# Rank products of two token groups later in the attention loop, the third group routed by VectorE, both halves of the second expert weights loaded behind the loop

## The reference

```python
h = mod(x_flat[:, :2].sum(axis=1).astype(int32), 8)     # route of each token
sel = stack([h, mod(h + 1, 8)], axis=1)                 # two experts per token
# for each expert e: acc += 0.5 * (relu(x @ W1[e] + b1[e]) @ W2[e] + b2[e]) where e in sel
```

## Time and profile before

| | us |
|---|---|
| median of 3 runs | 357.28 |
| lowest and highest | 352.55, 359.18 |
| the profiled execution | 350.9 |
| its span | 349.1 |
| PE busy | 267.8 (77%) |
| DVE busy | 174.5 (50%) |
| ACT busy | 152.4 (44%) |
| POOL busy | 121.7 (35%) |

### The profile page before, as it was taken

How to read it: one execution, slowest core, us unless ns; L and a number is a source line. 1 busy time by engine, 2 the same in 40 slices (tenths; PEclk the granted TensorE clock), 3 DMA queues, 4 the chain that set the end, 5 groups by cost and what they waited for, 6 DMA issues and landing times. The chain is left out here.

```text
span 349.1 us, 7349 instructions
## 1 busy us (share of the span) xinstructions
PE 267.8 (77%) x2443; PEld 205.1 (59%) x2443; DVE 174.5 (50%) x612; ACT 152.4 (44%) x367; POOL 121.7 (35%) x213
## 2 busy tenths in 40 slices
PE   0798966589699977898887969721078999999990
PEld 0587755345486755354545445421066999999990
DVE  4640656910315677787783913166001565665650
ACT  2234124438668664577673653301016343434430
POOL 4000015503305324264074553756000443534441
PEclk9999999879989999899997885555569999999997
DMA  7800005601998645278500000402792000000000
GB/s 215 261 6 1 0 5 142 127 0 47 227 182 257 145 110 93 77 151 202 125 3 18 18 4 25 128 8 84 157 243 61 8 23 15 17 15 15 7 15 13
DMA packets 30546, 28.34 MB, mean 81 GB/s; under 512 B 2846, under 2 KB 27041, under 8 KB 30515
## 3 DMA queue, kind: packets, MB, share of 16 engines
q1 hardware_dynamic: 28900, 25.24, 30.4%
q0 software_dynamic: 1328, 2.66, 2.3%
q10 hardware_dynamic: 288, 0.07, 0.1%
HBM read 17.85 MB, written 10.37 MB: 81 GB/s over the span
## 5 line engine op out<-in xcount | busy, mean ns | idle before, releaser
L980 ACT ACTIVATE CTX<-ps 128x512 f32<-128x512 f32 x64 | 37.5, 601 | 34.9 <-PE ps L656 27.1
L1162 DVE TENSOR_REDUCE M<-ps 128x4 f32<-128x512 f32 x64 | 42.7, 685 | 17.3 <-PE ps L621 17.0
L1020 ACT ACTIVATE KPK<-ps,EB 128x128 f32<-128x128 f32 x80 | 24.7, 359 | 41.7 <-PE ps L799 41.7
L799 PE MATMUL ps<-QPK,EW 128*128 x320 | 39.1, 275 | 0.8 <-ACT QPK L1005 0.8
L808 PE MATMUL ps<-EW,KPK 128*128 128x128 f32 x320 | 39.7, 277 | 0.0
L1325 DVE TENSOR_SCALAR KPK<-ps,EB 128x128 f32<-128x128 f32 x80 | 22.5, 345 | 33.7 <-PE ps L799 33.7
L808 PEld LDWEIGHTS ps<-EW,KPK 128*128 128x128 f32 x320 | 38.0, 191 | 0.0
L799 PEld LDWEIGHTS ps<-QPK,EW 128*128 128x128 f32 x320 | 37.3, 192 | 1.0 <-issue 1.0
L1487 POOL DMA_INDIRECT out_dram<-ADD,tok_u x21 | 21.0, 1001 | 44.1 <-DVE ADD L1318 44.1
L656 PE MATMUL ps<-QPK,KPK 49*128 49x128 bf16 x256 | 27.8, 236 | 5.4 <-DVE M L1162 2.6
L656 PEld LDWEIGHTS ps<-QPK,KPK 49*128 49x128 bf16 x256 | 16.1, 101 | 19.7 <-issue 15.0
(11 more groups left out here) (215 smaller groups left out, 546.0 us busy)
## 6 DMA issues: line engine op xcount, KB each, us to landing
k_packed_scratch<-PART SPq DMA_DIRECT2D x24, 128.0 KB, 2.4
KPK<-k_packed_scratch SPq DMA_DIRECT2D x8, 384.0 KB, 6.6
q_packed_scratch<-PART SPq DMA_DIRECT2D x24, 128.0 KB, 2.4
QPK<-q_packed_scratch SPq DMA_DIRECT2D x8, 384.0 KB, 5.8
KPK<-sorted_scratch SPq DMA_DIRECT2D x13, 198.0 KB, 4.1
EW<-in_eW_dram SPq DMA_DIRECT2D x1, 2048.0 KB, 13.4
sorted_scratch<-XW SPq DMA_DIRECT2D x8, 198.0 KB, 4.5
X<-in_x_dram SPq DMA_DIRECT2D x4, 256.0 KB, 4.4
```

Of the source, the lines that this page charges most:

```text
L799: last = mm(ps[:, c // 2, (c % 2) * P:(c % 2 + 1) * P], EW1[:, e, (c % NF) * P:(c % NF + 1) * P], XST[:, bass.ds((t + shift[h]) * P, P)], ...
L980: A(EXPS[:, u % 4, :], ps[:, 2 + u % 2, :], ACT.Exp).then_inc(s_exp, 1)
L1020: last = A(HE[:, c, :], ps[:, k, (c % 2) * P:(c % 2 + 1) * P], ACT.Relu, bias=EB1[:, h, c:c + 1])
L1162: nc.vector.tensor_reduce(M[:, b % RING, c:c + 4], bank_rows(u % 2), AX.X, ALU.max).then_inc(s_max, 1)
```

## The change

Five edits:

1. `ranks(0)` moves from the end of unit 39 to the end of unit 42, `ranks(1)` from unit 55 to unit 62. On DVE `place(0)` moves from unit 40 to unit 44 and `place(1)` from unit 56 to behind the loop. The `max_T` that waits for `s_ranked` is now that of unit 45.
2. Group 2 is normalised by DVE in unit 63; `whole_parts(2)` runs on DVE behind the loop ahead of the last two `attention_rows`, `experts(2)` and `count_experts(2)` behind them. POOL's `normalise_rows(2)` and `route(2)` go.
3. A semaphore `s_x2v` counts the groups that DVE normalised.
4. POOL's four DMAs of `scatter(0)` wait for units 46, 48, 50 and 52 of the scores (before: 41, 43, 45, 47), and those of `scatter(1)` for no unit any more.
5. Both halves of `EW2` are loaded behind the loop.

```diff
@@ sync @@
             sp.wait_ge(s_f2, G)
             eW2_rows = eW2.rearrange("e (c p) d -> p e c d", p=P)
-            sp.dma_start(EW2[:, 0:NE // 2, :, :], eW2_rows[:, 0:NE // 2]).then_inc(ld_exp, 16)
             sp.wait_ge(s_pv, 4 * B)
-            sp.dma_start(EW2[:, NE // 2:NE, :, :], eW2_rows[:, NE // 2:NE]).then_inc(ld_exp, 16)
+            for h in (0, NE // 2):
+                sp.dma_start(EW2[:, h:h + NE // 2, :, :], eW2_rows[:, h:h + NE // 2]).then_inc(ld_exp, 16)
@@ tensor @@
                 if r == 1 and b + 2 < B:
-                    if b > 2 * GB and b % GB == 2:
-                        pe.wait_ge(s_ranked, b // GB - 1)
+                    if b == 2 * GB + 3:
+                        pe.wait_ge(s_ranked, 1)
                     max_T(b + 2)
...
-                if r == 3 and b > 2 * GB and b % GB == 1:
-                    pe.wait_ge(s_negm, min(b + 3, B))
-                    ranks(b // GB - 2)
+                if u == 4 * (2 * GB + 2) + 2:
+                    pe.wait_ge(s_negm, b + 3)
+                    ranks(0)
+                if u == 4 * (3 * GB + 3) + 2:
+                    pe.wait_ge(s_negm, B)
+                    ranks(1)
...
-            pe.wait_ge(s_negm, B)
+            pe.wait_ge(s_ranked, G - 2)
             ranks(G - 2)
@@ vector @@
-                normalise(lambda b: X2[:, b, 0:P], lambda b: blk(N, b), 3, g, s_ers, s_x2)
+                normalise(lambda b: X2[:, b, 0:P], lambda b: blk(N, b), 3, g, s_ers, s_x2v)
...
-                dve.wait_ge(s_x2, g + 1)
+                dve.wait_ge(s_x2v, g - 1)
...
-                if r == 0 and b > 2 * GB and b % GB == 2:
-                    place(b // GB - 2)
+                if u == 4 * (3 * GB + 3) + 3:
+                    normalise_x2(2)
+                if u == 4 * (2 * GB + 3):
+                    place(0)
+            place(1)
+            whole_parts(2)
             attention_rows(B - 2)
             attention_rows(B - 1)
+            experts(2)
+            count_experts(2)
             add_x1(G - 1)
@@ gpsimd @@
-                pool.wait_ge(s_x2, g + 1)
+                pool.wait_ge(s_x2 if g < 2 else s_x2v, g % 2 + 1)
                 for b in range(g * GB, (g + 1) * GB):
-                    if g < 2:
-                        pool.wait_ge(s_sc, 16 * g + 41 + 2 * (b % GB))
+                    if g == 0:
+                        pool.wait_ge(s_sc, 46 + 2 * b)
...
-            normalise_rows(2)
-            route(2)
             scatter(2)
             scatter(3)
```

More of the change, by code:

```diff
@@ L279, in decoder_layer @@
         s_rd2 = sem("s_rd2"); s_on = sem("s_on")
-        s_oT = sem("s_oT"); s_oTs = sem("s_oTs"); s_pr = sem("s_pr"); s_y2 = sem("s_y2"); s_x2 = sem("s_x2")
+        s_oT = sem("s_oT"); s_oTs = sem("s_oTs"); s_pr = sem("s_pr"); s_y2 = sem("s_y2"); s_x2 = sem("s_x2"); s_x2v = sem("s_x2v")
         s_x2id = sem("s_x2id")
```

## The result

| | before | changed |
|---|---|---|
| median of 24 runs, us | 351.64 | 348.50 |
| lowest | 347.39 | 336.13 |
| highest | 363.15 | 362.29 |

The changed kernel is faster: ratio 0.969, 95% interval 0.964 to 0.974. The ratio compares, of each kernel, only the executions near its own fastest, which is why it says 11 us and the medians only 3. This gap between the two figures is the finding of this case. The forecast was 343, range 336 to 350.5. The forecast was counted from a median of 357.28 over 3 runs; over 24 runs the kernel before has 351.64.

A forecast was written before the change was run, and what follows sets the result against it. PE's two waits for POOL's counts, 5.3 us, and the half clock behind them were taken to delay the expert loop; 0.6 + 3.7 + 7.7 - 0.3 + 1.2 = 12.9 us off gave 344.4 from the 357.28 median, stated as 343, range 336 to 350.5.

The forecast's parts named there:

- Unit 56 to the end of the loop: PE's last units with ranks(1) seven units later: 8.9 us at full clock against 16.6, so 7.7 gained.
- `ranks(1)` in time: At unit 62, POOL's last count at 206.6 and PE there at about 207.3: 0.7 us to spare.
- `ranks(0)`: Three units later in the loop: 3.7 us gained from unit 46, with a new PE idle time of 1.1.
- The weights: First weight half out of the loop: 0.6 us gained, the wait for the row of maxima at unit 28.
- DVE at the loop's end: New DVE work makes attention_rows(14) 1.5 us late, full clock gives 1.2 back: net 0.3 lost.
- Group 2: Route off POOL, behind the loop: DVE has its counts before project(3) is done, 1.2 us gained.
- a cover: scatter(1) behind the loop costs nothing since scatter(2) can't start before 218.9; without that cover it would cost 5.1 us.
- The sum: All terms over the kernel: 0.6 + 3.7 + 7.7 - 0.3 + 1.2 = 12.9 us gained.
- Rival A: Clock falls anyway past unit 51, where PE does less: gain 8.0 us, time 349; chance 22%.
- Rival B: Wait moves to unit 45 or POOL is late at unit 62, and the clock falls behind it: 347.6 us; chance 12%.

The follow-up runs named there:

- fill_45: Changed kernel plus three filler products in unit 45, ahead of the wait that the change added; median 338.09 us, ratio 0.958 against the kernel before.
- half_in_loop: Changed kernel with the first half of the second expert weights loaded in the loop again, as before; median 346.9 us of 4 executions, no ratio.
- filled_before: Kernel before, with 12 warm-up products ahead of each of the two ranks products in the loop; median 347.90 us, ratio 0.988.
- after_again: The changed kernel run once more, unedited, for a second trace; median 348.98 us, 335.36 to 360.99 in 12 executions.
- group2_pool: Changed kernel with group 2 normalised and routed on POOL again, ahead of scatter(1); median 350.62 us, ratio 1.002 against the kernel before.

## Why the prediction was right or wrong

A trace of the changed loop whose clock holds is that of `fill_45` (span 335.8, against 349.1), and the forecast's sum can be read against it. PE in its last nine units, at the loop's end, and at the start of the expert loop:

```profile
198.46 0.39 PE L661 MATMUL ps<-QPK,KPK 49*128 49x128 bf16 x4
...
206.09 0.41 PE L711 MATMUL ps<-OH,C 128*128 128x32 f32 x2
...
206.98 1.18 PE L683 MATMUL ps<-CTX,EW 128*32 128x128 f32 x24
...
253.88 2.05 PE L808 MATMUL ps<-QPK,EW 128*128 x16 [0.77 <-ACT QPK L1014]
```

and POOL and DVE:

```profile
205.49 0.20 POOL L1468 TENSOR_TENSOR CUM<-CUM,OH 128x8 f32<-128x8 f32 x1
```

```profile
209.81 0.26 DVE L1176 RECIPROCAL RD<-ps 128x16 f32<-128x16 f32 x1
...
213.98 0.17 DVE L1230 TENSOR_TENSOR CUM<-CUM,OH 128x8 f32<-128x8 f32 x1
215.59 0.69 DVE L1184 TENSOR_TENSOR N<-ps,X 128x512 f32<-128x512 f32 x1 [1.45 <-PE ps L721]
...
217.38 0.16 DVE L1240 TENSOR_TENSOR rank<-ps,OH 128x32 f32<-128x32 f32 x1
```

- **Unit 56 to the end of the loop.** Unit 55 ends at 199.2, the loop at 208.2: 9.0 us. Forecast 8.9, and 16.6 before. Right.
- **`ranks(1)` in time.** POOL's counts at 205.69, PE there at 206.09: 0.4 us to spare, forecast 0.7. Right, and thin.
- **`ranks(0)`.** From the end of unit 39 to unit 46: 12.3 us before (182.90 to 195.22), 8.4 in `half_in_loop` (183.29 to 191.70). 3.9 gained, forecast 3.7. Right. PE's idle time there is 0.46 and 0.67, forecast 1.1 in one piece. Right in size.
- **The weights.** The wait of 0.56 us at unit 28 is in no trace without the load in the loop. With the load it is in two of three, the kernel before and `half_in_loop` (0.58); in `filled_before`, which issues the load at 161.37, PE does not wait there. So the load can cause the wait and need not, and no run shows the 0.6 us in the time.
- **DVE at the loop's end.** `attention_rows(14)` comes 1.6 us behind the loop's end, against 0.7: 1.0 lost, forecast 1.5. To `add_x1` it is 5.8 us, against 6.0: 0.2 gained, forecast 1.2; PE idles there, and the clock reads only 0.66 over 210 to 215 us. Net 0.8 lost, not 0.3.
- **Group 2.** DVE's counts at 214.15, `project(3)` later, no wait in front of `place(2)`. `add_x1` to the copy of the totals takes 9.3 us, against 10.7 before: 1.4, forecast 1.2. Right. That the route off POOL also protects `scatter(1)` was in the forecast as a cover, and its price was underestimated: 5.1 named, 6.9 between the two traces and 9 between the fastest executions with what follows from it.
- **The sum.** 12.9 forecast; 13.3 between the two spans, 12.0 between the two floors. The expert loop begins at 253.88, forecast 254.5. The trace is of a kernel with three more products; the fastest execution of the changed kernel itself is 1.6 us below that of `fill_45`.
- **Rival A**, the fall for lack of work past unit 51: did not come. The clock reads 1.00 over that stretch in every trace in which it entered it so, among them 215 to 220 us above. The page's rule on transposes (the Trainium skill, TensorE: Matmul & The Clock Gate, Part 4: PE-mode transpose), by which A's time would have come, is not borne out here: the stretch has its transposes, among scores and value products, and the clock held.
- **Rival B** was given 12% and a time of 347.6. It is what five of the seven traces above show; the median of the 36 executions is 348.8. Its price was too small all the same, 2.4 us of half clock up to unit 44 and 0.8 of waiting, and nothing for the units behind. From `max_T` of unit 45 to the loop's end `fill_45` takes 18.8 us (189.38 to 208.16) and `half_in_loop`, where the clock falls, 28.1 (191.49 to 219.54, last row below): 9.3 more. The 347.6 is near by luck, since it is counted from the 357.28; from 351.64 it would be 342.

```profile
218.03 1.51 PE L678 MATMUL ps<-CTX,EW 128*32 128x128 f32 x24
```

The kernel came out faster, as forecast, the median lies in the stated range, and the terms of the sum hold in a trace that keeps its clock. The median is in the range by luck in part. The forecast's own range, without the rivals, was 336.5 to 346.5. And the 343 came from a base 5.6 us too high: from 351.64 the sum of 12.9 gives 338.7, and the median lies 9.8 above that, not 5.5.

**The step that failed** is the one from the sum to the time. It read: "As the part removed (an idle time that drops the clock) is one that may differ between executions, slower ones may gain more". The opposite holds. In the kernel before, no execution of 51 has a clock above 0.905, so the two long waits seem to cost it in all of them, and the time is bunched near 350. The change takes these away and leaves a loop that is at full clock only as long as nothing drops it, and it adds 0.67 us of idleness in the very stretch where DVE already keeps PE waiting 0.46. The forecast had this wait with its size and priced it by its length, 1.1 us, where a fall costs some 10: the span of `half_in_loop`'s trace, which falls there, is 9.9 us above that of `fill_45`, part of it from its wait at unit 28 and an earlier fall near 140.

## What to carry to other kernels

A wait of PE has two prices: its length, and what it costs if the clock falls behind it. In this loop the waits were 1.1 us together and a fall behind them cost 7 to 9 us up to the loop's end (`after_again` and `half_in_loop` against `fill_45`). So where a change removes long waits and adds a short one, look first at what already idles next to it, and put a few harmless products in front of the wait if its place is fixed; with three of them the median was 338 over six executions, and with two more in unit 44 it was 340 over twelve, against 349 without. And look at the spread and the granted clock of many executions before one profile is taken for the kernel.

## What the hardware showed that was not expected

- In `after_again` the clock fell behind two waits of 0.46 and 0.67 us, 1.8 us apart, with PE shown busy 4.39 of the 5 us before them. In `group2_pool` the same two waits came behind the same 4.39 of 5 us, and the clock held.
- Once low, the clock stayed so for 16 to 44 us behind the falls near 155 us, and for 20 us or more behind those at unit 45, with PE shown busy in nearly all of it up to the loop's end: 5.00 of 5 at 160 to 200 us in the first trace of the changed kernel. Behind the falls near 140 us it was back within 4 us. The same loop, entered at full clock, held 1.00 with PE busy 4.5 of 5 us (`fill_45`, 190 to 195).
- A small DMA, the row of maxima of unit 16 (4 KB), took 6.07 us from its issue at 150.39 in the first trace of the changed kernel, beside the large transfers there.
- SP's load of one value into a register took up to 1.40 us in `group2_pool` while POOL scattered; of those behind the pads the first took 2.10 us, with no scatter any more, and the others 0.15.
